# An attention and aggregation kernel over one adjacency: the head's loads and constants placed anew, and the tables of order rewritten

## The chip, the cores and the metric

The kernel runs on one core of a Trainium2 chip. The metric is the device time of one execution in microseconds, the median of several runs. The engines are TensorE (PE in the profile), VectorE (DVE), ScalarE (ACT), GpSimd (POOL) and SyncE (SP). SP only issues DMAs here; ACT and POOL issue DMAs beside their own work. All of them run their own programs in order and wait for each other by semaphores.

## What is computed

There are 4096 nodes with 64 features (`x`), an integer adjacency of 4096 x 4096 (64 MB as it lies in memory), a table of 4096 entities `V` with 64 features, and small matrices. Cut to what matters, the reference is

```python
h = maximum(layernorm(x), 0)
s = h @ W @ a1;  t = V @ W @ a2                 # one number per row, one per column
scores = s[:, None] + t[None, :]
e = where(adj > 0, leaky_relu(scores, 0.2), -9e15)
x = x + elu(softmax(e, axis=1) @ V + h)         # first layer
h = maximum(layernorm(x), 0)
x = x + relu((adj.T @ h) @ U.T / adj.sum(axis=0)[:, None])   # second layer
```

## The kernel before

**Tiling.** The rows of the adjacency are cut into 33 blocks of 124 or 125 rows. They lie on the chip as 8-bit numbers (`adj_sb`), converted by the DMA that loads them. The blocks form five groups, `GROUPS`: (0, 3), (3, 9), (9, 17), (17, 25) and (25, 33). The first layer goes over the groups (stages 0 to 4), and in each over the 32 column chunks `c` of 128. One step `(i, c)` is called a tile here.

**A tile.** PE multiplies the block's chunk by a diagonal matrix of 2^26 with the row's shift below it (`bi`), which is the mask (L1153). On most tiles ACT first writes a relu of the scores into the same PSUM tile (`relu`, L686), PE adds the mask, and ACT takes the exponential (L668). On the tiles in `DVE_TILES` the mask is made alone, DVE joins it with the scores (`scores`, L884), and ACT takes the exponential of that (L672). Two tiles later PE multiplies the exponentials by `V` (`attend`, L1178).

**Guards.** Before a group can start, DVE must find for each of its rows the largest `t` among the row's neighbours: two halves for each block, in `guard` (L832). It reads the adjacency block (semaphore `adj_in[b]`) and `t_row`, which is `t` copied to all partitions. `row_shifts` (L857 to L876) turns the maxima into shifts, PE turns these over (`turn_halves`), ACT copies them (L625), and SP stores them into `bi` by two small DMAs (L372). While stage i runs, DVE makes the guards of group i+1, at the tiles that `GUARD_TILES[i]` names, one entry for each of them. The table `WHEN` names the tile at which every other piece of side work is issued, stage by stage: layer norm of group i+2 (`centre`, `squared`, `variance`, `scaled`), the closing work of group i-1 (`normalise`, `elu`, `square`, `high` and others), and the passing on of `s` (`sum_s`, `turn_s`, `copy_s`). Entries that end in `_0` are for group 1 in stage 0. An engine reaches a piece only after all that its own program has before it.

**The head.** Until the first guard, this runs: SP loads `W`, parts 1 and 3 of `V`, all of `x` and two copies of `U`; ACT loads `a`, and parts 0 and 2 of `V`. DVE forms `W a`, ACT and PE spread it over the partitions (`wa_row`, L599). `V` times that row is formed in four parts, two by POOL (L438) and two by DVE (`weighted`, L777), and DVE sums each (`sum_t`, L787) into `t_col`. PE runs 16 instructions that only keep it busy (L1052) once the first sum is there, and then turns over the smallest `t`, from which the shift comes (`shift_one`, L802 to L811), and makes the eight pieces of `t_row` (L1067); ACT copies six of them and DVE two (L816). DVE runs `centre(0)` (L748 to L752) and `variance(0)` in between. The constants of the mask, the diagonal of 2^26 in `bi` (L741) and in `turn` (L737), are made by DVE at its start.

**The adjacency's loads.** POOL issues them (L417), each behind a fill of the three rows below the block (L413, `set_ones`). It makes five fills first, then its two products for `V`, waits for parts 1 and 3 of `V`, and then issues the loads of blocks 0 to 4. The others follow in six places of POOL's program between other work.

**The second layer.** When the last tile's exponential is done, PE gathers `adj.T @ h` in eleven runs (`gather`, L1239), and DVE divides and adds.

## Time and profile before

| what | value |
|---|---|
| median of 3 runs | 386.7 us (385.74 to 387.5) |
| the profiled execution | 384.23 us |
| its span, first to last instruction | 382.4 us |
| busy: PE / DVE / ACT / POOL | 79% / 77% / 67% / 30% |
| DMA packets | 26809, 25.24 MB written |
| mean granted clock of TensorE | 0.958 of full |

The profile comes from one execution. Its time is 1.8 us more than its span, and 2.5 us below the median of the runs, so a difference is carried over from the profile to the median and not the time itself. A row of the timeline gives start, duration, engine, line, operation, output and inputs, and in square brackets how long the engine had been idle before it and what ended that. A row of the chain of waits gives start, duration and piece. In the rows on the DMA, q0 is POOL's queue, q1 is SP's and q10 is ACT's; the share is the time that its packets took, of 16 DMA engines.

### The profile page before, as it was taken

To read this page: it belongs to the slowest core of one execution; us is meant where nothing else is said; L and a number is where in the kernel's file an instruction comes from. 1 tells how busy PE (TensorE), PEld (TensorE's weight loads), DVE (VectorE), ACT (ScalarE), POOL (GpSimd) and SP (SyncE) were. 2 spreads that over 40 slices of the span, in tenths; PEclk is the share of its full clock that TensorE was granted. 3 is DMA by queue.
4 is the path that set the end of the run, shared out by engine and by line. 5 is a ranking of instruction groups with operands and counts; after the bars stand their busy time and mean duration, and the time that the engine had idled before them with its cause. 6 is when DMAs were issued, how large, how long until landed. Compare 5 with 4: busy or idle time off the path is not lost.

```text
span 382.4 us, 16263 instructions
## 1 busy us (share of the span) xinstructions
PE 302.1 (79%) x7582; PEld 279.3 (73%) x7582; DVE 295.1 (77%) x401; ACT 257.2 (67%) x318; POOL 115.4 (30%) x120
## 2 busy tenths in 40 slices
PE   1916766676778677868788977788989999999996
PEld 0812654576667667767778876678989999999996
DVE  7899999895999578797987798998988764008333
ACT  2312799879999988799989999986787871010000
POOL 8866486387220660030015120012111103010000
PEclk9967699869999999899999999999999999999999
DMA  9999999999999999996000001001110005101100
GB/s 167 135 107 110 108 108 111 137 106 109 110 144 105 102 111 105 101 105 111 3 4 3 3 22 39 2 3 38 26 32 3 3 5 110 30 3 42 34 22 19
DMA packets 26809, 25.24 MB, mean 66 GB/s; under 512 B 22041, under 2 KB 22105, under 8 KB 26742
## 3 DMA queue, kind: packets, MB, share of 16 engines
q0 software_dynamic: 4752, 16.90, 42.5%
q1 hardware_dynamic: 19830, 6.75, 7.9%
q8 instruction: 59, 0.97, 1.0%
q10 hardware_dynamic: 2160, 0.56, 0.8%
q14 instruction: 8, 0.07, 0.0%
HBM read 72.76 MB, written 2.11 MB: 196 GB/s over the span
## 4 chain that ended last, share of the span: by engine, by line
PE 35%; DVE 32%; issue 10%; ACT 10%; POOL 9%; DMA 3%; SPq 0%; POOLq 0%; DVEq 0%; ACTq 0%
DVE scratch L832 20%; PE w L1178 11%; PE q L1239 10%; PE q L1153 6%; PE w L1239 6%; DVE arena L884 5%; ACT q L686 4%; ACT arena L672 3%; ACT arena L668 3%; POOL adj_sb L413 2%; DMA bi<-rows_sb 2%; POOL buf_b L470 2%; POOL adj_sb L417 1%; PE w L1052 1%; POOL stat_c L513 1%
## 5 line engine op out<-in xcount | busy, mean ns | idle before, releaser
L1178 PE MATMUL w<-v_sb,arena 128*61 128x65 f32 (+1 forms) x4224 | 158.0, 225 | 6.7 <-issue 5.4
L832 DVE CUSTOM_DVE_ANT_0 scratch<-adj_sb,t_row 125x2048 uint8<-125x2048 uint8 x66 | 152.5, 2310 | 1.4
L1178 PEld LDWEIGHTS w<-v_sb,arena 128*64 128x64 f32 (+1 forms) x4224 | 143.0, 140 | 8.3 <-issue 6.0
L1153 PE MATMUL q<-bi,adj_sb 128*64 128x125 bf16 x2112 | 95.6, 226 | 45.6 <-ACT q L686 35.8
L1153 PEld LDWEIGHTS q<-bi,adj_sb 128*64 128x64 fp8e4 x2112 | 71.4, 113 | 60.7 <-ACT q L686 46.9
L668 ACT ACTIVATE arena<-q,t_col 128x1000 f32<-128x1000 f32 (+2 forms) x104 | 90.6, 874 | 8.5 <-PE q L1153 8.2
L672 ACT ACTIVATE arena<-arena,t 128x1000 f32<-128x1000 f32 (+2 forms) x56 | 61.3, 1094 | 16.2 <-DVE arena L884 15.5
L884 DVE SCALAR_TENSOR_TENSOR arena<-arena,b_col,q 128x1000 f32<-128x1000 f32 (+1 forms) x42 | 51.0, 1223 | 17.4 <-PE q L1153 13.5
L686 ACT ACTIVATE q<-second_row,minus_b 128x750 f32<-128x750 f32 (+1 forms) x50 | 49.0, 979 | 1.3
L686 ACT ACTIVATE q<-arena,minus_b 128x375 f32<-128x375 f32 (+1 forms) x54 | 43.5, 806 | 1.3
L1239 PE MATMUL q<-g_all,adj_sb 124*128 124x129 f16 (+1 forms) x660 | 39.1, 220 | 0.0
L1239 PEld LDWEIGHTS q<-g_all,adj_sb 124*128 124x128 fp8e4 (+1 forms) x660 | 38.6, 97 | 0.1
L413 POOL MEMSET adj_sb<- 32x1024 f32 x33 | 32.4, 981 | 0.6
L522 POOL TENSOR_TENSOR g_all<-buf_a,g_all 125x512 f16<-125x512 f32 (+2 forms) x5 | 5.4, 1075 | 80.3 <-ACT buf_a L662 80.3
L1239 PE MATMUL w<-g_all,adj_sb 124*128 124x129 f16 (+1 forms) x396 | 23.6, 220 | 0.0
L1019 DVE RECIPROCAL rdeg<-q 128x3 f32<-128x3 f32 (+1 forms) x7 | 1.2, 176 | 29.0 <-PE q L1239 29.0
L1239 PEld LDWEIGHTS w<-g_all,adj_sb 124*128 124x128 fp8e4 (+1 forms) x396 | 23.3, 97 | 0.0
L513 POOL TENSOR_TENSOR stat_c<-stat_b,minus_half 125x8 f32<-125x8 f32 (+2 forms) x5 | 13.1, 2627 | 32.7 <-DVE stat_b L935 32.7
L884 DVE SCALAR_TENSOR_TENSOR arena<-second_row,b_col,q 128x1000 f32<-128x1000 f32 (+1 forms) x14 | 16.4, 1180 | 8.5 <-PE q L1153 4.6
L417 POOL DMA_DIRECT2D adj_sb<-in_adj_dram x33 | 17.9, 545 | 8.3 <-POOL adj_sb L413 8.3
L505 POOL TENSOR_TENSOR buf_a<-x_sb,stat_a 125x512 f32<-125x512 f32 (+2 forms) x5 | 6.6, 1316 | 38.1 <-DVE stat_a L926 38.1
L458 POOL TENSOR_TENSOR stat_c<-stat_b,minus_half 125x8 f32<-125x8 f32 (+2 forms) x5 | 7.2, 1431 | 33.0 <-DVE stat_b L762 33.0
(139 smaller groups left out, 207.2 us busy)
## 6 DMA issues: line engine op xcount, KB each, us to landing
adj_sb<-in_adj_dram POOLq DMA_DIRECT2D x33, 500.0 KB, 40.7
arena<-s_dram SPq DMA_DIRECT2D x2, 500.0 KB, 7.1
out_dram<-v_sb SPq DMA_DIRECT2D x10, 96.0 KB, 1.8
x_sb<-in_x_dram SPq DMA_DIRECT2D x1, 928.0 KB
v_sb<-x_dram SPq DMA_DIRECT2D x1, 768.0 KB, 5.4
v_sb<-n_L_gnn_entity_embs_dram ACTq DMA_DIRECT2D x2, 256.0 KB, 5.7
v_sb<-n_L_gnn_entity_embs_dram SPq DMA_DIRECT2D x2, 256.0 KB, 4.7
second_row<-s_dram SPq DMA_DIRECT2D x1, 500.0 KB, 3.7
```

What stands on the lines that cost most here:

```text
L413: nc.gpsimd.memset(adj_words[96:P, b, :], FOUR_ONES).then_inc(ones_set, 1)
L417: nc.gpsimd.dma_start(adj_sb[0:R, b, :], adj[first_row(b):first_row(b) + R, :]).then_inc(adj_in[b], 16)
L470: nc.gpsimd.tensor_tensor((buf_a if i == 0 else buf_b)[0:R, 0:nb, :], g_sb[0:R, b0:b1, :], wa_row[0:R, 0:1, :].to_broadcast([R, nb, D]), A ...
L513: nc.gpsimd.tensor_tensor(stat_c[0:R, b0:b1], stat_b[0:R, b0:b1], minus_half[0:R, 0:b1 - b0], ALU.pow)\
L668: nc.scalar.activation(e_part(n, nb), part(q[n % Q_SLOTS], nb), ACT.Exp, bias=t_col[:, c:c + 1])\
L672: nc.scalar.activation(e_part(n, nb), e_part(n, nb), ACT.Exp, bias=t02[:, c:c + 1])\
L686: nc.scalar.activation(part(q[n % Q_SLOTS], nb), a_part(i, nb), ACT.Relu, bias=minus_b[:, c:c + 1]).then_inc(relued, 1)
L832: nc.vector.tensor_tensor_reduce(out=junk[0:R, :], in0=adj_bytes[0:R, b, half], in1=t_row[0:R, half], scale=1.0 / ONE, scalar=0.0, op0=ALU ...
L884: nc.vector.scalar_tensor_tensor(out=e_part(n, nb), in0=a_part(i, nb), scalar=b_col[:, c:c + 1], in1=part(q[n % Q_SLOTS], nb), op0=ALU.max ...
L1153: last = nc.tensor.matmul(q[n % Q_SLOTS][e:e + width, bank, start:start + R], weights, bi[:, i % BI_SLOTS, k, :], start=not ON_ACT[n] and ...
L1178: last = nc.tensor.matmul(att(i)[e0:e1, bank, place_in, :], e[:, k * R + e0:k * R + e1], v_sb[:, c, :], start=(c == 0 and place_in == 0), ...
L1239: done = nc.tensor.matmul(out_bank(o)[:, (c - c0) * (2 * D + 1):(c - c0 + 1) * (2 * D + 1)], adj_sb[0:rows, b, c * P:(c + 1) * P], h2[0:ro ...
```

## The change

**Loads of `x`.** `x` has a semaphore for each group. SP loads group 0 first, then `U`, then groups 1 and 3 and the long rows of group 4 (blocks 29 to 32). Group 2 and the rest of group 4 (blocks 25 to 28) are loaded by ACT, which issues these two DMAs after its copies of `t_row`. `centre(i)` waits for its group.

**The constants.** The diagonals of `bi` are made by ACT, behind its copies of `wa_row`; that of `turn` by DVE, after it has split `t`. The copy of the identity to bf16 comes first on DVE.

**`V` times the row.** POOL forms part 0 alone. DVE forms parts 1, 3 and 2, and sums 1, 3, 0, 2 in between. POOL then waits for parts 3 and 2 of `V` and issues the adjacency's loads.

**The shift.** PE multiplies the shift to all partitions after one of the eight pieces of `t_row` and not after two (`SHIFT_AT`).

**The tables.** DVE has three more tiles: (1, 26), (1, 30) and (2, 18). `GUARD_TILES` and `WHEN` are new in a number of places; among them, layer norm of group 2 starts with `centre` at tile 18 of stage 0 and not 8, that of group 1 at tile 7 and not 0, and the scaling of `U` on DVE is at tile 4 and not 7.

```diff
...
     DVE_TILES = [(29, 31),
-                 (25, 27, 29, 31),
-                 (1, 7, 9, 12, 22, 27, 29, 30, 31),
+                 (25, 26, 27, 29, 30, 31),
+                 (1, 7, 9, 12, 18, 22, 27, 29, 30, 31),
                  (1, 3, 6, 8, 10, 12, 28, 29, 30, 31),
...
-    GUARD_TILES = [(7, 8, 10, 11, 12, 15, 15, 16, 18, 19, 20, 22),
-                   (0, 2, 3, 4, 4, 6, 6, 9, 9, 10, 15, 16, 18, 20, 21, 22),
-                   (4, 6, 6, 10, 10, 13, 14, 15, 15, 21, 21, 21, 22, 23, 24, 26),
-                   (4, 9, 10, 12, 13, 17, 17, 17, 17, 19, 21, 21, 21, 23, 23, 24)]
+    GUARD_TILES = [(6, 8, 10, 10, 11, 13, 14, 16, 18, 20, 20, 21),
+                   (0, 0, 2, 3, 4, 6, 6, 11, 11, 13, 15, 18, 20, 20, 21, 23),
+                   (4, 6, 6, 10, 10, 13, 14, 15, 16, 19, 20, 21, 22, 23, 24, 26),
+                   (4, 9, 10, 12, 13, 17, 17, 17, 18, 19, 20, 21, 21, 23, 24, 24)]
...
         'elu': (None, 4, 7, 3, 8),
-        'elu_below': (None, 7, 7, 6, 8),
-        'square': (None, 15, 11, 10, 11),
+        'elu_below': (None, 7, 7, 7, 8),
+        'square': (None, 14, 11, 10, 11),
         'spread': (None, 12, 12, 12, 13),
         'scale': (None, 17, 14, 14, 16),
-        'turn_h2': (None, 20, 17, 18, 18),
+        'turn_h2': (None, 20, 16, 18, 18),
         'copy_h2': (None, 20, 17, 18, 18),
-        'times_u': (None, 22, 19, 25, 21),
+        'times_u': (None, 23, 19, 25, 21),
         'high': (None, 24, 21, 26, 21),
         'sum_s': (11, 2, 4, 2, None),
-        'range': (24, 26, 28, 24, None),
+        'range': (24, 26, 27, 24, None),
         'turn_r': (27, 27, 30, 28, None),
         'copy_r': (27, 27, 29, 27, None),
-        'centre': (8, 1, 3, None, None),
-        'squared': (23, 26, 28, None, None),
+        'centre': (18, 1, 3, None, None),
+        'squared': (24, 26, 28, None, None),
         'variance': (28, 27, 30, None, None),
         'scaled': (31, 30, 31, None, None),
-        'centre_0': (0, None, None, None, None),
-        'squared_0': (1, None, None, None, None),
+        'centre_0': (7, None, None, None, None),
+        'squared_0': (4, None, None, None, None),
         'variance_0': (8, None, None, None, None),
...
         'reduce_v': (3, None, None, None, None),
-        'square_u': (3, None, None, None, None),
-        'scale_u': (7, None, None, None, None),
+        'square_u': (2, None, None, None, None),
+        'scale_u': (4, None, None, None, None),
         'turn_u': (1, None, None, None, None),
-        'copy_u': (2, None, None, None, None),
+        'copy_u': (4, None, None, None, None),
         'turn_s': (13, 11, 9, 10, None),
-        'copy_s': (15, 7, 19, 12, None),
+        'copy_s': (15, 10, 19, 12, None),
     }
...
     TINY = 1e-30
+    SHIFT_AT = 1
...
     T_ON_ACT, T_ON_DVE = (0, 2, 4, 5, 6, 7), (1, 3)
-    LN_PARTS = [(0, 1), (1, 9), (9, 17), (17, 25), (25, 33)]
...
         v_in = [sem(f"v_in{i}") for i in range(PARTS)]
-        x_in = sem("x_in")
+        x_in = [sem(f"x_in{i}") for i in range(NI)]
+        bi_set = sem("bi_set")
...
             load_v(3)
-            sp.dma_start(x_sb[:, 0:SHORT, :], x_short).then_inc(x_in, 16)
-            sp.dma_start(x_sb[0:R, SHORT:NB, :], x[EDGE:N, :].rearrange("(k p) d -> p k d", p=R)).then_inc(x_in, 16)
+            def load_x(i):
+
+                b0, b1 = GROUPS[i]
+                sp.dma_start(x_sb[:, b0:b1, :], x_short[:, b0:b1, :]).then_inc(x_in[i], 16)
+
+            load_x(0)
             for h in range(2):
                 sp.dma_start(u_sb[:, h * D:(h + 1) * D], U[:, :]).then_inc(u_in, 16)
+            for i in (1, 3):
+                load_x(i)
+            sp.dma_start(x_sb[0:R, SHORT:NB, :], x[EDGE:N, :].rearrange("(k p) d -> p k d", p=R)).then_inc(x_in[NI - 1], 16)
...
                 elif b == ONES_FIRST:
-                    pool.wait_ge(v_weighted_pool, 2)
+                    pool.wait_ge(v_weighted_pool, 1)
                 elif b == 7:
...
             pool.wait_ge(ones_set, ONES_FIRST)
-            for k in (0, 2):
-                chunks = slice(k * NC // PARTS, (k + 1) * NC // PARTS)
-                pool.wait_ge(v_in[k], 16)
-                pool.wait_ge(wa_rows_copied, 2)
-                if k == 0:
-                    pool.wait_ge(consts, 6)
-                else:
-                    pool.wait_ge(v_weighted_pool, 1)
-                nc.gpsimd.tensor_tensor(v_wa[:, chunks, :], v_sb[:, chunks, 0:D],
-                                        wa_row[:, 1:2, :].to_broadcast([P, NC // PARTS, D]), ALU.mult).then_inc(v_weighted_pool, 1)
-            for k in (1, 3):
+            chunks = slice(0, NC // PARTS)
+            pool.wait_ge(v_in[0], 16)
+            pool.wait_ge(wa_rows_copied, 2)
+            pool.wait_ge(consts, 6)
+            nc.gpsimd.tensor_tensor(v_wa[:, chunks, :], v_sb[:, chunks, 0:D],
+                                    wa_row[:, 1:2, :].to_broadcast([P, NC // PARTS, D]), ALU.mult).then_inc(v_weighted_pool, 1)
+            for k in (3, 2):
                 pool.wait_ge(v_in[k], 16)
...
                     .then_inc(wa_rows_copied, 1)
+            act.wait_ge(consts, 2)
+            act.wait_ge(consts_dve, 2)
+            for s in range(BI_SLOTS):
+                nc.scalar.activation(bi[0:R, s, :, :], ident[0:R, 0:R].unsqueeze(1).to_broadcast([R, 8, R]), ACT.Copy, scale=BIG)\
+                    .then_inc(bi_set, 1)
             act.wait_ge(t_summed, PARTS)
...
                     .then_inc(t_copied_act, 1)
+            for i, (b0, b1) in ((2, GROUPS[2]), (4, (GROUPS[4][0], SHORT))):
+                act.dma_start(x_sb[:, b0:b1, :], x_short[:, b0:b1, :]).then_inc(x_in[i], 16)
...
                 act.wait_ge(shifts_turned, 1)
+                act.wait_ge(bi_set, BI_SLOTS)
                 nc.scalar.activation(bi[96:P, 0, 0:nb, :].rearrange("p b c -> p (b c)"), first_rows()[96:P], ACT.Copy)\
...
             dve.wait_ge(consts, 2)
-            nc.vector.tensor_scalar(turn[0:R, 0:3, 0:29], ident[0:R, 96:R].unsqueeze(1).to_broadcast([R, 3, 29]), BIG, None, ALU.mult)\
-                .then_inc(consts_dve, 1)
-            dve.wait_ge(consts_dve, 3)
-            for s in range(BI_SLOTS):
-                nc.vector.tensor_scalar(bi[0:R, s, :, :], ident[0:R, 0:R].unsqueeze(1).to_broadcast([R, 8, R]), BIG, None, ALU.mult)\
-                    .then_inc(consts_dve, 1)
+            nc.vector.tensor_copy(ident16[:, :], ident[:, :]).then_inc(consts_dve, 1)
...
                 mean, part_x = stat_a[0:R, b0:b1], x_sb[0:R, b0:b1, :]
+                dve.wait_ge(x_in[i], 32 if i == NI - 1 else 16)
                 nc.vector.tensor_reduce(mean, part_x, AX.X, ALU.add).then_inc(sum1_done, 1)
...
                 chunks = slice(k * NC // PARTS, (k + 1) * NC // PARTS)
-                if k % 2 == 1:
-                    dve.wait_ge(v_weighted_dve, k // 2 + 1)
+                if k == 0:
+                    dve.wait_ge(v_weighted_pool, 1)
                 else:
-                    dve.wait_ge(v_weighted_pool, k // 2 + 1)
+                    dve.wait_ge(v_weighted_dve, {1: 1, 3: 2, 2: 3}[k])
                 nc.vector.tensor_reduce(t_col[:, chunks], v_wa[:, chunks, :], AX.X, ALU.add).then_inc(t_summed, 1)
...
-            nc.vector.tensor_copy(ident16[:, :], ident[:, :]).then_inc(consts_dve, 1)
             weighted(1)
+            sum_t(1)
+            weighted(3)
+            sum_t(3)
+            weighted(2)
             sum_t(0)
-            weighted(3)
-            sum_t(1)
             sum_t(2)
-            sum_t(3)
             dve.wait_ge(t_summed, PARTS)
...
             nc.vector.tensor_tensor(t_lo, t_col[:, :], t_hi, ALU.subtract).then_inc(t_split, 1)
+            nc.vector.tensor_scalar(turn[0:R, 0:3, 0:29], ident[0:R, 96:R].unsqueeze(1).to_broadcast([R, 3, 29]), BIG, None, ALU.mult)\
+                .then_inc(consts_dve, 1)
             dve.wait_ge(t_min_turned, 1)
...
                                            op0=ALU.mult, op1=ALU.max).then_inc(shift_one_done, 1)
-            dve.wait_ge(x_in, 32)
             centre(0)
...
             pe.wait_ge(t_split, 1)
-            pe.wait_ge(consts_dve, 2 + 1 + BI_SLOTS + 1)
+            pe.wait_ge(consts_dve, 3)
             for g in range(NG):
-                if g == 2:
+                if g == SHIFT_AT:
                     pe.wait_ge(shift_one_done, 1)
...
                 pe.wait_ge(a_copied, 1)
+                pe.wait_ge(consts_dve, 4)
                 nb = GROUPS[0][1] - GROUPS[0][0]
...
                     pe.wait_ge(bi_made, 1)
+                    pe.wait_ge(bi_set, BI_SLOTS)
                 if c == 0 and i >= 1:
...
                 if ON_ACT[n]:
...
```

## Rows read from the trace of the kernel before

**Rows 1.** The page: shares of the chain that ended last, by engine.
```profile
PE 35%; DVE 32%; issue 10%; ACT 10%; POOL 9%; DMA 3%; SPq 0%; POOLq 0%; DVEq 0%; ACTq 0%
```

**Rows 2.** Busy time by stretch: length, then PE, PEld, DVE, ACT, POOL, clock, DMA.
```profile
160.00:180.00 20.00, 15.61 (x441) 13.92 (x438) 18.37 (x19) 19.26 (x21) 3.26 (x1) 1.00 0.91 112
```

**Rows 3.** The chain of waits, the head: start, length, piece.
```profile
4.97 1.86 DVE bi L741 x2
...
10.22 3.79 PE w L1052 x16
...
15.19 1.02 DVE stat_a L750
...
19.04 2.29 DVE scratch L832
```

**Rows 4.** Timeline of DVE in the head.
```profile
8.89 0.68 DVE L777 TENSOR_TENSOR arena<-v_sb,wa_row 128x512 f32<-128x512 f32 x1
...
10.09 1.06 DVE L777 TENSOR_TENSOR arena<-v_sb,wa_row 128x512 f32<-128x512 f32 x1
11.08 1.86 DVE L787 TENSOR_REDUCE t_col<-arena 128x8 f32<-128x512 f32 x3
12.97 0.19 DVE L797 TENSOR_REDUCE columns<-t_col 128x1 f32<-128x32 f32 x1
```

**Rows 5.** Timelines of ACT, POOL and SP in the head.
```profile
1.36 1.48 ACTq L575 DMA_DIRECT2D v_sb<-n_L_gnn_entity_embs_dram  x2
...
6.44 0.34 ACT L599 ACTIVATE wa_row<-w 128x64 f32<-128x64 f32 x2 [1.26 <-PE w L1047]
...
26.36 0.48 ACT L631 ACTIVATE arena<-w 128x375 f32<-128x375 f32 x1 [5.90 <-PE w L1125]
...
7.40 1.49 POOL L438 TENSOR_TENSOR arena<-v_sb,wa_row 128x512 f32<-128x512 f32 x1
...
10.55 2.84 POOL L417 DMA_DIRECT2D adj_sb<-in_adj_dram  x5
...
3.81 5.79 SPq L353 DMA_DIRECT2D x_sb<-in_x_dram  x1
```

**Rows 6.** DMA: q1 in 10 to 11 us; q0 and q1 in 18 to 20 us.
```profile
q1 hardware_dynamic: 851, 0.22, 134.1%
...
q0 software_dynamic: 54, 0.20, 97.7%
q1 hardware_dynamic: 53, 0.01, 4.9%
```

**Rows 7.** DMA issues, us to landing: block 0 alone, then the first five (median).
```profile
adj_sb<-in_adj_dram POOLq DMA_DIRECT2D x1, 500.0 KB, 8.2
...
adj_sb<-in_adj_dram POOLq DMA_DIRECT2D x5, 500.0 KB, 17.3
```

**Rows 8.** Timeline of DVE: two guards, block 2's first and the ninth of stage 0.
```profile
29.23 2.29 DVE L832 CUSTOM_DVE_ANT_0 scratch<-adj_sb,t_row 125x2048 uint8<-125x2048 uint8 x1
...
60.86 2.29 DVE L832 CUSTOM_DVE_ANT_0 scratch<-adj_sb,t_row 125x2048 uint8<-125x2048 uint8 x1
```

**Rows 9.** Timelines of DVE and ACT: the end of stage 1.
```profile
125.14 1.00 DVE L884 SCALAR_TENSOR_TENSOR arena<-second_row,b_col,q 128x750 f32<-128x750 f32 x1 [0.37 <-PE q L1159]
...
127.31 0.27 ACT L625 ACTIVATE rows_sb<-w 16x125 bf16<-16x125 f32 x1
```

**Rows 10.** The chain of waits, the end of stage 1.
```profile
128.34 5.97 DMA bi<-rows_sb
```

**Rows 11.** Timelines of ACT and DVE, stage 2.
```profile
169.66 1.10 ACT L686 ACTIVATE q<-arena,minus_b 128x1000 f32<-128x1000 f32 x1
170.70 1.08 ACT L668 ACTIVATE arena<-q,t_col 128x1000 f32<-128x1000 f32 x1
...
183.66 1.13 ACT L672 ACTIVATE arena<-arena,t 128x1000 f32<-128x1000 f32 x1
...
182.29 1.26 DVE L884 SCALAR_TENSOR_TENSOR arena<-arena,b_col,q 128x1000 f32<-128x1000 f32 x1 [2.83 <-PE q L1153]
```


## The prediction, made before the changed kernel had run

> **What bounds the kernel now.** I read the chain of waits first, then the head's timelines, then the busy time by stretch, then the queues. The chain goes through PE and DVE for two thirds of its length [rows 1], and no stage in it is free: the head runs on DVE and PE to 19.0, where the first guard starts [rows 3]; stages 0 and 1 follow DVE's guards; in stage 2 ACT is busy for 19.26 of 20 us [rows 2]; the end is PE's. So time saved early counts only if DVE, the adjacency and ACT all let it through.
>
> In the head, DVE makes the two diagonals of `bi` from 4.97 on [rows 3], though `wa_row` is there by 6.8 [rows 5], and weighs its first part of `V` only at 8.89 [rows 4]. The last sum ends at 12.94 and the smallest `t` is taken at 12.97. PE's 16 filler instructions start at 10.22 and take 3.79 [rows 3], so PE can turn over the smallest `t` only at 14.0. A stop of DVE follows, the mean of `x` at 15.19 with 1.02 us for 125x3 elements [rows 3].
>
> The loads have a timetable of their own. Block 0 is issued at 10.55 [rows 5] and lands 8.2 later, at 18.8; the median of the first five is 17.3 us [rows 7], which is block 2, issued about 11.7 and so landing about 29.0. DVE asks for block 2 at 29.23 [rows 8]. So in group 0 guards and loads arrive together: a faster DVE alone gains nothing there.
>
> **DVE's part of the head.** What goes from DVE's start: 2.88 us of diagonals, of which the chain shows 1.86 before the work behind it. What comes: one product for `V`, at 0.68 to 1.06 us [rows 4]. The new order from 6.85 is product 1, sum 1, product 3, sum 3, product 2, sum 0, sum 2. Three products at 0.68 and four sums at 0.62 (1.86 for three [rows 4]) are 4.5 us, so the smallest `t` starts at 11.4 and not 12.97, if nothing stops DVE. If product 3 has to wait until POOL's product ends at 8.9 [rows 5], 0.7 is added and it is 12.1. PE's filler starts after sum 1, at about 8.2, and ends at 12.0, not 14.0. PE can thus turn `t` over at 12.0 to 12.5, 1.3 to 1.8 earlier. Behind that DVE has the diagonal of `turn`, a few tenths, partly in its wait for PE. The shift is multiplied after one piece of `t_row`; it was behind the mean of `x` anyway, so this is worth nothing by itself. The mean can again stop for up to 1 us: POOL's second fill behind the loads falls at about 13.7, where the mean stands now. I take the stop as it was; without it 0.9 more comes. First guard: 1.4 earlier, at 17.6 (bounds 0.7 and 2.2).
>
> The one-microsecond stop ends where POOL's fill ends, as the trace has it. The Trainium skill, SBUF — State Buffer, section on the two separate sides, says that VectorE and GpSimd share one pair of ports as an exclusive lock, also for a VectorE operation with two SBUF inputs against a GpSimd one that reads SBUF. By that rule a second VectorE product beside POOL's waits it out whole, and the smallest `t` starts at 12.1; the trace agrees only in part (one product took 0.68 beside POOL's, one took 1.06 [rows 4]).
>
> **ACT's part.** Two diagonals on ACT: 2 x 1.1 us, estimated by the 128x1000 relu at 1.10 [rows 11], from 6.8 to 9.0. The next thing there waits for the sums, beyond 11.4, so they cost nothing; if the cover were gone, their 2.2 us would stand before the first guard. Two DMA issues come after the copies of `t_row`: two of twice the size together took 1.48, but SP was once held for 5.79 by one issue [rows 5]. ACT's next wait, for PE and the first row of scores, was 5.90 long [rows 5] and keeps that length, so both ends fit and I cost it at nothing; `copy_rows` and everything else of ACT is queued behind it.
>
> **The loads.** POOL drops its second product, 1.5 us, and issues from about 9.0, 1.6 earlier than 10.55 [rows 5]. Parts 2 and 3 of `V` were used before the first loads were issued and are not later now. SP keeps 2804 packets behind `V` (group 0, `U`, groups 1 and 3, the long rows) where there were 4340. At 851 in a microsecond [rows 6] the 1536 missing ones are 1.8 us of the queue, so SP's share is done when the adjacency begins. Blocks 0 and 2 land at 17.2 and 27.4.
>
> The 1536 packets come back beside the adjacency. In 18 to 20 us POOL's queue moved 54 packets and SP's 53 [rows 6]: they alternate, and SP's took 4.9% of 16 engines, 0.030 us each (0.049 x 2 x 16 / 53). From about 20 to 27 that is some 190 packets, 0.35 us on block 2. It lands at 27.8, and DVE wants it at 29.23 - 1.4 = 27.8. Group 0 so ends 1.2 to 1.4 earlier, and the load of block 2 is late next. Later blocks have over a microsecond to spare, also with the 2.9 us (1536 x 0.030 / 16) that the small packets take in all.
>
> **Stage 0.** Of its side work only the order changes: one `centre` of eight blocks moves from before guard 5 to behind guard 9, `U` is scaled before the first guard, where DVE may wait some 0.1 for POOL. The sum for DVE is the same. I carry 1.4 to stage 1 (bounds 0.7 and 2.2).
>
> **Stage 1.** ACT is relieved of two tiles, but DVE's guards set its end, and one score of 1.00 us (tile 26) now stands between the last guard and `row_shifts`. DVE had 0.37 of idle just behind them [rows 9]. The copy of the shifts on ACT at 127.31 [rows 9] and SP's small DMA of 5.97 us [rows 10] hang on this. Bounds: the whole 1.00 is lost, or nothing. I take 0.5 as lost, between the 0.63 that this idle leaves and the ease that ACT gets in front of its copy: 0.9 is left at the start of stage 2.
>
> **Stage 2.** Tile 18 falls where ACT is full. There it costs relu and exponential, 1.10 + 1.08; afterwards only 1.13 [rows 11]: 1.05 less. DVE has 1.26 more and had 2.83 of idle before tile 22 [rows 11]. The last guards start behind tile 22, so they come 1.0 earlier too (bounds: nothing, if PE was what held tile 22, and 1.1). The rest of the tables shifts entries by a tile or two; nothing for it, bounds 0.5 either way. Stages 3 and 4 and the gather keep their length.
>
> **Sum.** 1.4 - 0.5 + 1.0 = 1.9 us. The profiled execution would be 382.3 instead of 384.2; on the median, 386.7 - 1.9 = 384.8.
>
> **Rivals.**
> 1. *Group 2's `x` lands late* (slower). Its 1024 packets alternate with the adjacency's from about 20. `centre(2)` stands behind the ninth guard, which ended at 63.15 [rows 8]; less 1.4 and less the 1.5 of the moved `centre` that is 60.3. At 27 packets in a microsecond [rows 6] they need 38 us, landing at 58; it decides against the change when the rate is under 1024 / 40 = 25. At 22 it lands at 66.5 and DVE stands for 6.2 us with all guards of group 1 behind it: 386.7 - 1.9 + 6.2 = 391.0; at 24, 2.4 us more and 387.2. At 23, 4.2 more: 389.0, which I take as its price. For it: there is hardly any reserve, and the last of 16 engines counts. Against it: 53 beside 54.
>    The Trainium skill, DMA: Bandwidth & Descriptors, section on queues, rings and completion order, says that each engine goes round the queues packet by packet; the trace agrees (53 beside 54). By it the rate is that of the adjacency's packets, and `x` is in time.
> 2. *The head's gain is lost before stage 2.* Stage 1 loses the whole 1.0, or blocks 1 and 2 come later, since the early rows of `x` also delay them; what is left is stage 2's 1.0 and a few tenths: 385.8. For it: DVE and loads are level in group 0, and the 5.97 us of the small DMA vary.
> 3. *More than the sum.* The mean of `x` is not stopped, stage 1 loses nothing: 2.2 + 1.0 + 0.4 of the tables: 383.1.
> 4. *ACT is held by its two issues* for longer than 5.9 us. Against it: 1.48 for twice as many packets. It would end as rival 2 or slower.
>
> **Chances.** Forecast 0.47, rival 1 0.13, rival 2 0.22, rival 3 0.15, rival 4 0.03. What a measurement of this kernel can tell from no change is 0.5%, 1.9 us: faster is below 384.8. The forecast lies on that line, and I give it 0.29 to faster and 0.18 to same; with rival 3 faster is 0.44. Same: 0.18, rival 2 and 0.01 of rival 4, 0.41. Slower: rival 1 and the rest, 0.15. The range goes from 382.7 (rival 3 with its bounds) to 388.4 (rival 1 for the greater part).
>
> **What the profile would show.** The first product for `V` on DVE near 6.9; the smallest `t` at 11.4 to 12.3; the filler on PE at 8.2; the first adjacency issue at 9.0, landing by 17.3; the first guard at 17.6 and block 2's at 27.8. ACT's wait before its first copied row stays over 3 us. No idle of DVE before `centre(2)` near 60, else rival 1. Tile (1, 26)'s score before `row_shifts`, and the copy of shifts near 126.4, else rival 2. Tile 22 of stage 2 some 2 us earlier. The prediction is wrong if the first guard does not move by a microsecond, or if a gain that is there at stage 2 is gone at the gather.

## The result and the profile after

The changed kernel takes 387.38 us (median of 22 runs, 385.57 to 388.71), the kernel before 385.95 beside it (22 runs, 383.62 to 387.5). The ratio is 1.0034, with a 95% interval of 1.0019 to 1.005: slower by 1.4 us. 384.8 was predicted, 1.9 us less than the 386.7 of before from which the prediction started. The profiled execution took 387.07 us, its span is 385.3. The one of before was itself 1.7 us under its median of 22 runs; a second trace of that kernel was of an execution of 387.09, so single traces of it differ by 2.9 us. What the second trace was expected to show:

> The kernel before, unchanged, for a second trace: the first was 1.7 us faster than the median of its kernel. All theories expect the same times to about 0.2 us at the first guard (19.0) and at the start of stage 1, and 0 to 2.5 us later at the end of stage 2 (the last row_shifts of stage 2 at 194 to 196.5), Theory C in the form of longer idle of TensorE by issue (7.4 us in 36 to 206 in the first trace, 9 to 12 here).

It came out so: first guard at 19.03, the last `row_shifts` of stage 2 at 195.69, and 11.8 us of "issue", where the first trace has 7.7.

The page of after, the busy time of each engine and the shares of the chain that ended last:

```profile
PE 302.0 (78%) x7590; PEld 279.0 (72%) x7590; DVE 295.4 (77%) x403; ACT 256.5 (67%) x317; POOL 113.2 (29%) x119
...
PE 38%; DVE 24%; ACT 20%; issue 8%; DMA 5%; POOL 4%; SPq 1%; DVEq 0%; POOLq 0%
```

No engine has notably less or more to do. DVE's share of the chain is 24% where it was 32% [rows 1], ACT's 20% where it was 10%; but the second trace of before has 21% and 20%, so this can't be put down to the change.

The head's times are near the predicted ones. After, timeline of DVE from the first product to the first guard:

```profile
6.35 0.69 DVE L785 TENSOR_TENSOR arena<-v_sb,wa_row 128x512 f32<-128x512 f32 x1 [1.34 <-DMA v_sb<-n_L_gnn_entity_embs_dram]
7.08 0.69 DVE L795 TENSOR_REDUCE t_col<-arena 128x8 f32<-128x512 f32 x1
8.66 0.69 DVE L785 TENSOR_TENSOR arena<-v_sb,wa_row 128x512 f32<-128x512 f32 x1 [0.89 <-DMA v_sb<-n_L_gnn_entity_embs_dram]
...
11.89 0.19 DVE L805 TENSOR_REDUCE columns<-t_col 128x1 f32<-128x32 f32 x1
12.00 0.81 DVE L806 CAST scratch<-t_col 128x32 bf16<-128x32 f32 x1
...
13.99 0.59 DVE L758 TENSOR_SCALAR stat_a<-stat_a 125x3 f32<-125x3 f32 x1
...
17.42 2.29 DVE L841 CUSTOM_DVE_ANT_0 scratch<-adj_sb,t_row 125x2048 uint8<-125x2048 uint8 x1
```

The first product starts at 6.35, where it was 8.89 [rows 4]; the smallest `t` at 11.89, where it was 12.97; the first guard at 17.42, where it was 19.04 [rows 3]. POOL's fill, at 11.82 for 0.95, now falls beside the cast at 12.00, which takes 0.81. After, timelines of POOL, ACT and PE in the head:

```profile
8.94 2.84 POOL L425 DMA_DIRECT2D adj_sb<-in_adj_dram  x5 [0.72 <-DMA v_sb<-n_L_gnn_entity_embs_dram]
...
6.13 1.97 ACT L608 ACTIVATE bi<-ident 125x1000 bf16<-125x1000 f32 x2
...
17.47 0.37 ACTq L621 DMA_DIRECT2D x_sb<-in_x_dram  x1
...
17.88 0.62 ACTq L621 DMA_DIRECT2D x_sb<-in_x_dram  x1
...
24.74 0.48 ACT L643 ACTIVATE arena<-w 128x375 f32<-128x375 f32 x1 [5.90 <-PE w L1135]
...
7.82 3.78 PE L1061 MATMUL w<-ident 128*128 128x128 f32 x16 [1.95 <-DVE t_col L795]
```

The adjacency's first load goes out at 8.94. ACT's diagonals end at 8.1, its two issues took 0.99 us, and its wait is still 5.90. Rival 4 is out.

**Where the lead goes.** The start of a group's `row_shifts` on DVE (L857 before, L866 after) marks the end of its guards. From the timelines of DVE, us:

| kernel | first guard | group 0 | group 1 | group 2 | group 3 |
|---|---|---|---|---|---|
| before | 19.04 | 33.90 | 70.20 | 123.33 | 194.06 |
| before, second trace | 19.03 | 34.12 | 70.47 | 123.57 | 195.69 |
| after | 17.42 | 32.25 | 68.92 | 123.46 | 196.92 |

The lead of 1.6 is still 1.3 to 1.5 when stage 0 ends. It is gone at the end of stage 1, and stage 2 is 1.3 to 2.7 us longer. Tile 22 of stage 2, which should have come 2 us earlier, is 2.9 later than in the first trace of before and 1.4 later than in the second (183.76). After, timeline of DVE at the end of stage 1, then at tile 22 of stage 2:

```profile
121.50 2.04 DVE L893 SCALAR_TENSOR_TENSOR arena<-second_row,b_col,q 128x750 f32<-128x750 f32 x2
123.46 0.16 DVE L866 TENSOR_TENSOR g_max<-g_max 125x8 f32<-125x8 f32 x1
...
185.16 1.26 DVE L893 SCALAR_TENSOR_TENSOR arena<-arena,b_col,q 128x1000 f32<-128x1000 f32 x1 [1.96 <-PE q L1164]
```

The two scores in front of `row_shifts` are those of tiles 25 and 26. The score at 185.16 waited for PE. What did PE wait for? The waits of PE from 138 to 182 us (columns: engine and line, releaser, us in all, times, the longest), first before:

```profile
PE w L1178 <- issue: 4.8, 4, 2.0
PE q L1153 <- ACT q L686: 3.5, 6, 1.0
PE q L1153 <- issue: 1.1, 2, 0.8
```

and after:

```profile
PE w L1189 <- issue: 4.8, 4, 2.6
PE q L1164 <- ACT q L698: 4.7, 6, 1.5
PE w L1216 <- DVE rows_sb L858: 2.0, 1, 2.0
PE q L1164 <- issue: 0.4, 1, 0.4
```

In before, 5.9 of the 9.4 us in which PE stood are "issue": nothing that the profile records held it. In after it is 5.2, and the 2.0 before L1216, which have DVE's name, turn out below to be of the same kind. The stops come some 6 us apart, also inside a tile. Before, timeline of PE: 32 equal matmuls of one `attend`, of which the last 19 come 2 us late:

```profile
154.63 0.78 PE L1178 MATMUL w<-v_sb,arena 128*64 128x65 f32 x19 [2.00 <-issue]
```

The DMA view has a queue of its own kind for this. From 96 to 187 us its line is the same before and after (packets, MB, share of 16 engines):

```profile
q8 instruction: 16, 0.26, 1.0%
```

These are 16 packets of 16 KB in 91 us. From 96 to 182 us PE ran 1865 matmuls and 1861 weight loads in before; over 15 packets that is 250 instructions a packet, so q8 brings PE's program. The starts of its packets, from the trace, in us from the span's start:

| kernel | 4th | 6th | 21st | mean distance, 6th to 21st |
|---|---|---|---|---|
| before | 65.9 | 85.5 | 176.6 | 6.08 |
| before, second trace | 65.9 | 85.6 | 178.0 | 6.16 |
| after | 62.3 | 85.1 | 177.1 | 6.13 |

The expectation for the changed kernel with the wide mask, further down, has the packets of 96 to 182 us; it counts from the start of the DMA record, 10.5 to 10.6 us before the first instruction. The 4th packet comes 3.6 us earlier after the change, the 6th 0.4. From there to the end of the adjacency's load (its last packet starts at 179) they come about 6.1 us apart; behind that, the 22nd to 28th of before are 3.3 to 5.3 apart.

Do these packets end PE's stops? The longest stop of each trace, and the one that has DVE's name:

| kernel | PE stood for | a packet of q8 ended | PE went on |
|---|---|---|---|
| before | 2.00 (issue) | 153.41 | 154.63 |
| before, second trace | 2.27 (issue) | 154.90 | 156.25 |
| after | 2.56 (issue) | 153.57 | 155.06 |
| after | 2.02 (`<-DVE rows_sb`) | 178.03 | 179.28 |

It is so for all of them. The traces of before, after and experiments 1 to 4 have 71 "issue" stops from 36 to 206 us, and each ends 1.20 to 1.59 us behind the end of a packet of q8. PE's waits of over 0.8 us for ACT or for the row's DMA, in the same traces from 119 to 190 us, end 4.8 to 6.3 us behind one. So PE stands there until its next instructions are in.

When does this bind? In those seven traces no "issue" stop before 119 us is longer than 0.2 us, though the packets come as far apart; from 119 to 186 us, the end of stage 1 and stage 2, there are up to 12 in a trace. This is theory C, on which the experiments turn, as far as the traces bear it: in stage 2 the supply of PE's instructions sets a pace that neither head nor tables can beat, while new delays are added to it. Stage 1 is not paced by it.

The Trainium skill, Runtime: NRT & Kernel Launch, section on instruction fetch mechanics, says that an engine fetches blocks of 256 instructions through a DMA queue of its own while it runs the present block, and that the crossing is mostly hidden. The blocks are there in the trace; hidden they are not, beside the adjacency's load, at 5.9 us in the 44 from 138 to 182 us.

### The profile page after: what moved, and what is told of

It is laid out like the page before. It is cut to its first block, busy times and chain, and to the rows that moved or that the text cites. A ratio compares the mean times of both kernels' runs of the same rounds, so it can differ in the third digit from the quotient of the medians.

```text
span 385.3 us, 16284 instructions
## 1 busy us (share of the span) xinstructions
PE 302.0 (78%) x7590; PEld 279.0 (72%) x7590; DVE 295.4 (77%) x403; ACT 256.5 (67%) x317; POOL 113.2 (29%) x119
## 4 chain that ended last, share of the span: by engine, by line
PE 38%; DVE 24%; ACT 20%; issue 8%; DMA 5%; POOL 4%; SPq 1%; DVEq 0%; POOLq 0%
DVE scratch L841 14%; PE w L1189 11%; PE q L1250 10%; ACT q L698 9%; ACT arena L680 8%; PE q L1164 7%; PE w L1250 6%; DVE arena L893 5%; DMA bi<-rows_sb 4%; ACT arena L684 3%; DMA v_sb<-n_L_gnn_entity_embs_dram 2%; PE w L1085 2%; POOL stat_c L517 1%; PE w L1216 1%; POOL stat_c L462 1%
## 5 line engine op out<-in xcount | busy, mean ns | idle before, releaser
L680 ACT ACTIVATE arena<-q,t_col 128x1000 f32<-128x1000 f32 (+2 forms) x101 | 87.8, 872 | 7.9 <-PE q L1164 7.8
L684 ACT ACTIVATE arena<-arena,t 128x1000 f32<-128x1000 f32 (+2 forms) x59 | 64.2, 1089 | 22.0 <-DVE arena L893 21.3
L893 DVE SCALAR_TENSOR_TENSOR arena<-arena,b_col,q 128x1000 f32<-128x1000 f32 (+1 forms) x43 | 52.3, 1224 | 20.1 <-PE q L1164 15.1
L698 ACT ACTIVATE q<-second_row,minus_b 128x750 f32<-128x750 f32 (+1 forms) x48 | 47.2, 983 | 1.3
L698 ACT ACTIVATE q<-arena,minus_b 128x375 f32<-128x375 f32 (+1 forms) x53 | 42.4, 800 | 1.2
L893 DVE SCALAR_TENSOR_TENSOR arena<-second_row,b_col,q 128x1000 f32<-128x1000 f32 (+1 forms) x16 | 18.4, 1156 | 7.9 <-PE q L1164 4.6
L517 POOL TENSOR_TENSOR stat_c<-stat_b,minus_half 125x8 f32<-125x8 f32 (+2 forms) x5 | 13.1, 2617 | 31.4 <-DVE stat_b L944 31.4
L462 POOL TENSOR_TENSOR stat_c<-stat_b,minus_half 125x8 f32<-125x8 f32 (+2 forms) x5 | 9.1, 1821 | 34.3 <-DVE stat_b L770 34.3
```

Source lines behind the costliest of these rows:

```text
L462: nc.gpsimd.tensor_tensor(stat_c[0:R, b0:b1], stat_b[0:R, b0:b1], minus_half[0:R, 0:b1 - b0], ALU.pow)\
L517: nc.gpsimd.tensor_tensor(stat_c[0:R, b0:b1], stat_b[0:R, b0:b1], minus_half[0:R, 0:b1 - b0], ALU.pow)\
L680: nc.scalar.activation(e_part(n, nb), part(q[n % Q_SLOTS], nb), ACT.Exp, bias=t_col[:, c:c + 1])\
L684: nc.scalar.activation(e_part(n, nb), e_part(n, nb), ACT.Exp, bias=t02[:, c:c + 1])\
L698: nc.scalar.activation(part(q[n % Q_SLOTS], nb), a_part(i, nb), ACT.Relu, bias=minus_b[:, c:c + 1]).then_inc(relued, 1)
L893: nc.vector.scalar_tensor_tensor(out=e_part(n, nb), in0=a_part(i, nb), scalar=b_col[:, c:c + 1], in1=part(q[n % Q_SLOTS], nb), op0=ALU.max ...
```

## The experiments

**Without the wide mask.** All four ran beside each other and 35 runs of before (385.92 us).

1. `copy_s` of stage 2 earlier, for the stop of 2.0 us above, where PE seems to wait for DVE's copy into `rows_sb`:

```diff
-        'copy_s': (15, 10, 19, 12, None),
+        'copy_s': (15, 10, 15, 12, None),
```

> The changed kernel with one entry moved: the copy of s for group 3 stands at tile 15 of stage 2 and not at 19, so ahead of the guard at 16, the new VectorE tile 18 and the guard at 19. Theory A (VectorE reaches that copy late; TensorE stands 2.02 us at times_u for it and then runs at half clock, with all of stage 2 behind): the wait is gone and tile 22 comes about 2.9 us earlier than in the changed kernel; 387.4 - 2.9 = 384.5 us, ratio to before 0.995 to 0.998. Theory B (the rows of x loaded beside the adjacency make the later loads and the small DMAs slow, and the loss sits there): nothing moves, ratio 1.002 to 1.005.

Measured: 387.58 us, 1.0029 (1.0002 to 1.0055), as the change. DVE's copy now ended at 172.62 and no longer at 178.65. Its timeline of PE:

```profile
181.01 0.92 PE L1216 MATMUL w<-uu,buf_b 128*125 128x128 f32 x6 [2.05 <-issue]
```

The stop stays and changes its name. It ends 1.24 us behind a packet of q8, as it did in the changed kernel; the releaser named there was only the last to arrive that the view shows. Theory A fell.

2. Tile 18 of stage 2 back on ACT:

```diff
-                 (1, 7, 9, 12, 18, 22, 27, 29, 30, 31),
+                 (1, 7, 9, 12, 22, 27, 29, 30, 31),
```

> The changed kernel with tile (2, 18) back on ScalarE, all else kept, the guard at tile 19 too. Theory A: VectorE loses the 1.66 us wait and the 1.25 us score in front of the copy of s, which ends near 175.8 and not 178.7, before TensorE wants it at 177.3; ScalarE has its 1.05 us back. 387.4 - 2.9 + 1.05 = 385.5, ratio 0.998 to 1.000. Theory B: no better than the changed kernel, and worse by ScalarE's 1.05: ratio 1.003 to 1.007.

Measured: 386.63 us, 1.0000 (0.9975 to 1.0025). The tile was predicted as a gain of 1.0; taking it back gives 0.75, with intervals that overlap. It is no gain here. The ratio is one that theory A gave, whose mechanism experiment 1 had just taken away.

3. The new head and the new stage 0, with the entries of stages 1 to 4 as before:

```diff
-                 (25, 26, 27, 29, 30, 31),
-                 (1, 7, 9, 12, 18, 22, 27, 29, 30, 31),
+                 (25, 27, 29, 31),
+                 (1, 7, 9, 12, 22, 27, 29, 30, 31),
...
-        'copy_s': (15, 10, 19, 12, None),
+        'copy_s': (15, 7, 19, 12, None),
```

> The new head with the new entries of stage 0, and the tables of stages 1 to 4 as before. Theory A: what the head gives (1.6 us at the first guard, of which the trace still has 0.4 to 1.3 in stage 1) arrives: 384.7 to 385.6, ratio 0.9965 to 0.999. Theory B: the head's gain is eaten by slower DMAs: ratio 1.000 to 1.004.

Measured: 386.35 us, 1.0004 (0.9977 to 1.0031). The head alone moves nothing.

4. The code of before with all new tables (`DVE_TILES`, `GUARD_TILES`, `WHEN`):

```diff
-                 (25, 27, 29, 31),
-                 (1, 7, 9, 12, 22, 27, 29, 30, 31),
+                 (25, 26, 27, 29, 30, 31),
+                 (1, 7, 9, 12, 18, 22, 27, 29, 30, 31),
...
-        'centre': (8, 1, 3, None, None),
+        'centre': (18, 1, 3, None, None),
...
```

> The kernel before with the new tables alone: head, loads and constants as before. Theory A: the whole loss of stage 2 without the head's gain, 1.0 to 2.9 us: ratio 1.003 to 1.0075. Theory B: the tables are harmless: ratio 0.998 to 1.002.

Measured: 387.82 us, 1.0051 (1.0023 to 1.0079). The tables carry the loss.

**Fewer instructions of PE.** One number halves the mask's matmuls in stages 1 and 2: for each block one with 128 columns of weights and not two with 64. It was put into both kernels:

```diff
-    MASK_COLUMNS = (64, 64, 64, 64, 64)
+    MASK_COLUMNS = (64, 128, 128, 64, 64)
```

> The changed kernel with the mask of stages 1 and 2 multiplied 128 columns at a time and not 64: TensorE has 60 and not 72 instructions for a tile of stage 1 and 80 and not 96 for one of stage 2. Theory C: while the adjacency is loaded, a page of 256 TensorE instructions arrives only each 6.1 us (the instruction queue's packets in the traces of before and after lie 6.07 and 6.14 us apart from 96 to 182 us, and 4.6 to 4.7 apart later), TensorE stands idle for 0.4 to 2.6 us at the page's end, and what the other engines gain is taken back there. Then fewer instructions free stage 2: its idle by issue (5 to 10 us in the traces so far) falls below 2 us, 387.4 - 3 to - 5 = 382.4 to 384.4, ratio 0.990 to 0.996, and the head's gain shows against the next kernel. Theory A (VectorE reaches the copy of s late): ratio stays 1.002 to 1.005.

> The kernel before with the same wider mask in stages 1 and 2. Theory C: it also gains, by less than the changed kernel, as it starts 1.6 us later: 385.9 - 1.5 to - 3.5, ratio 0.991 to 0.996, and 1 to 1.6 us above the run before this. Theory A, or a TensorE that is slower with wide weights: ratio 1.000 or more, and the run before this is 1.4 us above it, as without the wide mask.

Measured: the changed kernel 382.45, 0.9918 (0.9898 to 0.9939); before 381.20, 0.9882 (0.9865 to 0.9899). Both gain, as theory C had it; but before was expected 1 to 1.6 us above the changed kernel and is 1.25 below, so no gain of the change was hidden. Before with this mask, the waits of PE from 138 to 182 us, all of them:

```profile
PE q L1153 <- ACT q L686: 6.0, 12, 1.0
```

Every "issue" stop is gone; from 86 to 177 us q8's packets are 5.7 to 8.1 us apart, 6.9 in the mean, so PE asks for them more slowly than it did. Is it the supply, or does the wide mask save PE's own time? The same width in all stages:

```diff
-    MASK_COLUMNS = (64, 64, 64, 64, 64)
+    MASK_COLUMNS = (128, 128, 128, 128, 128)
```

> Before with 128 columns of weights for the mask in all stages, not in 1 and 2 alone. Theory C (TensorE's instructions are fetched too slowly while the adjacency loads, until about 182 us): in stage 0 DVE's guards set the pace and in stages 3 and 4 the loading is over, so it gains little on the 0.9882 of stages 1 and 2 alone: 0.986 to 0.988. Rival (the wide mask saves TensorE's own time, whatever the fetch): stages 3 and 4, where TensorE is on the path, gain as much again as stages 1 and 2 did: 0.976 to 0.982.

Measured: 389.01 us, 1.0073 (1.0048 to 1.0097), 8 us over the version above. Both expectations missed. Busy time by stretch (PE first, instructions in brackets), in stage 1, before and then with the mask wide in stages 1 and 2:

```profile
96.00:123.00 27.00, 20.55 (x582) 17.98 (x578) 26.65 (x30) 26.26 (x37) 6.33 (x3) 1.00 1.00 120
```

```profile
96.00:123.00 27.00, 22.65 (x487) 18.57 (x488) 26.65 (x29) 26.42 (x37) 6.29 (x3) 1.00 1.01 120
```

In stage 3, with the mask wide in stages 1 and 2:

```profile
190.00:260.00 70.00, 56.98 (x1692) 52.38 (x1688) 61.99 (x76) 63.94 (x67) 14.96 (x10) 1.00 0.04 11
```

and in all stages:

```profile
190.00:260.00 70.00, 60.62 (x1422) 52.87 (x1418) 61.37 (x78) 63.49 (x66) 15.11 (x10) 1.00 0.03 10
```

PE is busy 3.6 us longer with 270 matmuls fewer, and 2.1 us longer with 95 fewer in stage 1. The wide mask costs PE time of its own in both, so it doesn't gain by saving PE's work: the rival of theory C is out. It gains in stage 2 alone (67.0 and 68.3 us in two traces, where the two of before have 70.7 and 72.1), and not in stage 1 (53.4 where it was 53.1). Of the 6.7 us between the two traces 0.6 are lost in stage 3 and 5.8 behind it, in stage 4 and the gather.

**With the wide mask: is the change worth something once PE is fed?**

The head and stage 0 (as 3, and the mask), then the tables alone (as 4, and the mask):

> The new head and stage 0 with the tables of stages 1 to 4 as before, and the mask of stages 1 and 2 made with 128 columns of weights a matmul in place of two of 64. Without the stops of TensorE's instruction supply, the old head and old tables gave a ratio of 0.9882, the whole change 0.9918. Theory D (the head is a gain that the supply hid): 1.0 to 1.5 us under that version of before, a ratio of 0.984 to 0.986. Rival (the packets of x beside the adjacency cost at the small DMA into bi what the head gained): 0.3 us under to 0.5 over it, 0.987 to 0.990. If it is 0.991 or more, the new head itself is the loss.

> The code of before with all the new tables, and the same wide mask. Theory D: the tables carry the whole penalty of some 1.3 us and more, since a faster head has to be made good too: 1.3 to 2.6 us over before with the wide mask, a ratio of 0.9915 to 0.995. Rival (the tables cost only through the supply of instructions): 0.988 to 0.990, as before with the wide mask.

Measured: 381.81, 0.9892 (0.9864 to 0.9919), and 383.02, 0.9922 (0.9895 to 0.9949). The first falls on its rival, a head that is worth nothing, the second on theory D, tables that cost. The changed kernel with the mask and tile 18 back on ACT, and before with the mask and two tiles of stage 1 on DVE:

> The changed kernel with the wide mask (0.9918) and tile 18 of stage 2 back on ScalarE. Theory F (the tile on VectorE delays the copy behind it, for which TensorE waits 1.0 us at the product with U): that wait is gone and it gains 0.4 to 1.0 us, a ratio of 0.989 to 0.9907. Rival (without the stops of the supply the tile is a gain, as the prediction had it, since ScalarE sets the pace of stage 2): it loses 0.3 to 1.0 us, 0.9925 to 0.9945.

```diff
-                 (25, 27, 29, 31),
+                 (25, 26, 27, 29, 30, 31),
```

> Before with the wide mask (0.9882) and tiles 26 and 30 of stage 1 moved to VectorE, no other entry. Theory G: the score of tile 26 stands between the last guard and the shifts of the next row, so that these start 0.7 to 1.0 us later and stage 2 as much later: 0.990 to 0.9908. Rival (stage 2 takes its pace from elsewhere, or ScalarE's relief pays it back): 0.9875 to 0.989.

Measured: 381.90, 0.9909 (0.9878 to 0.9941), and 382.50, 0.9918 (0.9887 to 0.995), the first between its two sides, the second over both. Last, stage 2's entries alone, the same with the new head, and the mask alone again:

```diff
-                 (1, 7, 9, 12, 22, 27, 29, 30, 31),
+                 (1, 7, 9, 12, 18, 22, 27, 29, 30, 31),
...
-        'turn_h2': (None, 20, 17, 18, 18),
+        'turn_h2': (None, 20, 16, 18, 18),
...
-        'range': (24, 26, 28, 24, None),
+        'range': (24, 26, 27, 24, None),
```

> Before with the wide mask of stages 1 and 2 and the new entries of stage 2 alone (tile 18 to VectorE, the guards of group 3, two steps one tile earlier). Theory: without the stops of the supply ScalarE and VectorE set stage 2's pace, as the prediction had it, and the entries are worth the 0.6 us by which stage 2 was shorter in the traces with all new tables (66.5 against 67.1 us): 0.4 to 1.0 us under before with the wide mask, which runs beside it. Rival: nothing, within 0.2 per cent of it.

> The same with the new head and the new stage 0: the change without its entries of stages 1, 3 and 4. Theory (the head keeps 0 to 0.7 us of its lead at stage 1, the two tiles of stage 1 were the loss): 0 to 0.7 us under the version without the new head, the best of all. Rival (blocks and x of group 2 arrive too late for the head to pay at all): equal to it or up to 0.6 us over.

> Before with the wide mask of stages 1 and 2 once more, as the measure for the two beside it, in more rounds: 0.987 to 0.990 of before.

Measured: 381.55, 0.9906 (0.9872 to 0.9939); 382.33, 0.9903 (0.9873 to 0.9934); 382.09, 0.9909 (0.9879 to 0.9938; 0.987 to 0.990 was expected). All these lie between 381.2 and 383.0, and nearly all of their intervals overlap: the wide mask is worth some 1%, and no part of the change can be told from nothing on top of it. In the first pair the change was 1.25 us slower than before also with the mask; the repeat of before (382.09 after 381.20) takes most of that back. Before with the mask beats before by 0.9 to 1.2%, and the changed kernel by more, and nothing beside it was measurably faster.

The traces say more than the times. Ends of the guards as in the table above, and the distance from group 1 to group 2 (stage 1) and from 2 to 3 (stage 2):

| kernel, with the mask | first guard | group 1 | stage 1 | stage 2 |
|---|---|---|---|---|
| before | 19.49 | 70.65 | 53.40 | 67.04 |
| new head and stage 0 | 17.57 | 70.42 | 53.39 | 67.31 |
| two tiles of stage 1 | 18.84 | 70.50 | 54.27 | 66.77 |
| tables alone | 19.01 | 70.41 | 54.43 | 66.44 |
| the change | 17.44 | 70.11 | 54.89 | 66.59 |
| the change, tile 18 back | 17.02 | 69.51 | 54.26 | 68.02 |
| before, a second measurement | 19.36 | 70.49 | 53.36 | 68.28 |
| stage 2's entries alone | 19.03 | 70.18 | 53.09 | 66.30 |
| the same with the new head | 19.04 | 70.44 | 53.37 | 68.39 |

*Stage 1.* The two tiles alone make it 0.87 us longer. DVE with the mask alone, then with the two tiles:

```profile
123.14 0.99 DVE L884 SCALAR_TENSOR_TENSOR arena<-second_row,b_col,q 128x750 f32<-128x750 f32 x1
124.05 0.16 DVE L857 TENSOR_TENSOR g_max<-g_max 125x8 f32<-125x8 f32 x1
```

```profile
122.96 1.90 DVE L884 SCALAR_TENSOR_TENSOR arena<-second_row,b_col,q 128x750 f32<-128x750 f32 x2
124.77 0.16 DVE L857 TENSOR_TENSOR g_max<-g_max 125x8 f32<-125x8 f32 x1
```

One score more stands before the shifts, and its whole length is lost. The other traces bear it out: stage 1 takes 54.2 to 55.4 us in the eight that have the two tiles, with and without the mask, and 53.1 to 53.4 in the eight others of this table, of before and of experiment 3.

*Stage 2.* With PE fed, the change has a stage 2 that is 1.4 us shorter than with tile 18 back on ACT (66.59 against 68.02). But two traces of one kernel, before with the mask, differ by as much (67.04 and 68.28), and the fourth with the tile on DVE has 68.39. The mean of the four with it is 66.9, that of the five without 67.5. A gain of some half a microsecond may be there; the predicted 1.05 is not shown, nor is any in the time.

*The head.* Its lead is 1.9 at the first guard and 0.2 at group 1. The trace of the version with head and stage 0 shows one cause, on DVE:

```profile
61.41 0.69 DVE L756 TENSOR_REDUCE stat_a<-x_sb 125x8 f32<-125x512 f32 x1 [0.66 <-DMA x_sb<-in_x_dram]
```

`centre(2)` waits 0.66 us for its `x`, in experiment 1 0.45 at 62.08; in the six other traces with the new head and the new stage 0 it did not wait. Elsewhere blocks came late. Experiment 3, timeline of DVE:

```profile
17.09 2.29 DVE L841 CUSTOM_DVE_ANT_0 scratch<-adj_sb,t_row 125x2048 uint8<-125x2048 uint8 x1 [1.37 <-DMA adj_sb<-in_adj_dram]
...
23.18 2.29 DVE L841 CUSTOM_DVE_ANT_0 scratch<-adj_sb,t_row 125x2048 uint8<-125x2048 uint8 x1 [0.50 <-DMA adj_sb<-in_adj_dram]
```

**Does `x` have to be moved at all?** First, experiment 3 with all of `x` issued by SP ahead of the adjacency, in pieces:

```diff
-            for i in (1, 3):
+            for i in (1, 2, 3):
                 load_x(i)
+            sp.dma_start(x_sb[:, GROUPS[4][0]:SHORT, :], x_short[:, GROUPS[4][0]:SHORT, :]).then_inc(x_in[4], 16)
...
-            for i, (b0, b1) in ((2, GROUPS[2]), (4, (GROUPS[4][0], SHORT))):
-                act.dma_start(x_sb[:, b0:b1, :], x_short[:, b0:b1, :]).then_inc(x_in[i], 16)
```

> The new head with stages 1 to 4 as before (1.0004 when last run), but all of x is issued by SyncE in the head: nothing of x is loaded beside the adjacency. If the 1536 small packets beside the adjacency cost what was lost between the first guard (1.6 us early) and the start of stage 1 (0.35 to 0.5 early), 0.9 us comes back at the small DMA into bi: ratio 0.998. If the early start of the adjacency is worth more, the first two blocks land up to 1.8 us later and VectorE waits for block 1 or 2: ratio 1.000 to 1.003. Theory C: whichever of these holds at stage 1 is levelled in stage 2, ratio 0.999 to 1.001.

Measured: 401.23 us (394.14 to 407.48; before 385.76 beside it), 4% slower, and its two fastest runs are still 2.6% slower (1.0257, 1.0217 to 1.0298). None of the expected ratios held. Its chain of waits:

```profile
57.05 27.56 DMA s_dram<-rows_sb
84.61 0.02 issue
84.62 9.76 DMA second_row<-s_dram
```

SP's small store of stage 1's row took 27.56 us, in SP's queue behind packets of `x` that were still there: 159 small packets of q1 in the 27 us from 57 to 84. Then the new head with SP's loads and all tables as before, and the wide mask:

```diff
+            sp.dma_start(x_sb[:, 0:SHORT, :], x_short).then_inc(x_in[0], 16)
+            sp.dma_start(x_sb[0:R, SHORT:NB, :], x[EDGE:N, :].rearrange("(k p) d -> p k d", p=R)).then_inc(x_in[0], 16)
```

> The new head on ScalarE, VectorE and GpSimd, but x loaded by SyncE in one piece behind V, as before, and all tables as before; the mask of stages 1 and 2 with 128 columns, to compare with 0.9882 (before with that mask) and 0.9892 (the new head with the new stage 0 and that mask). Theory E: the head's lead was lost in stage 0, because the mean of x for group 2 had to go behind the ninth guard, and GpSimd's power of group 1 then stands beside a guard of VectorE and takes 3.29 us in place of 1.33. With the mean back in front, the power takes 1.3 to 1.7, stage 1 begins 1.2 to 1.8 us earlier, and the time is 1.0 to 1.6 us less than before with the mask: 0.984 to 0.9856. Rival: the lead is lost to the loads, which begin beside the packets of x: the first guards of group 0 wait for adjacency blocks by 1 us or more, and the ratio is 0.987 to 0.990; if the store of stage 1's row lands over 10 us after its issue, over 1.0.

Of its 12 runs seven took 406 to 416 us and five 382.8 to 384.3; the ratio of the five is 0.9946 (0.9914 to 0.9978). The trace is of one of the seven. DVE, at the mean of `x` in the head:

```profile
48.75 0.35 DVE L747 TENSOR_REDUCE stat_a<-x_sb 125x3 f32<-125x192 f32 x1 [34.53 <-DMA x_sb<-in_x_dram]
```

and its queues from 14 to 42 us:

```profile
q0 software_dynamic: 822, 2.90, 99.2%
q1 hardware_dynamic: 355, 0.09, 2.3%
```

355 of SP's packets take 28 us, and `x` lands behind still more of them. The first load went out at 9.46 here, at 10.55 in before [rows 5]. One wait more holds it back:

```diff
             for k in (3, 2):
                 pool.wait_ge(v_in[k], 16)
+            pool.wait_ge(v_weighted_dve, 3)
```

> The version with the new head and x loaded in one piece as before (first adjacency load issued at 9.46, where before issues it at 10.55), with one wait more: GpSimd issues the first load only when VectorE's third product of V is done, at about 11.2. Theory H (an adjacency load that starts while the packets of x are still queued leaves some engines with one packet of x for each long one of the adjacency, and x lands 30 us late): with the loads held x lands by 15 us, no run is over 390 us, the first guard waits for block 0 until 19.3 to 19.7, and the time is that of before with the wide mask, 380.5 to 383.5 us. Rival (the late landing comes from something else in the new head): again more than a third of the runs over 395.

Measured: 382.31 us, 0.9901 (0.9867 to 0.9935), no run over 383.1; `x` by 15 and no run over 390 is what theory H had. The timelines of POOL and DVE:

```profile
11.20 2.84 POOL L418 DMA_DIRECT2D adj_sb<-in_adj_dram  x5 [2.58 <-DVE arena L777]
...
13.82 0.35 DVE L748 TENSOR_REDUCE stat_a<-x_sb 125x3 f32<-125x192 f32 x1 [0.80 <-DMA x_sb<-in_x_dram]
...
19.16 2.29 DVE L833 CUSTOM_DVE_ANT_0 scratch<-adj_sb,t_row 125x2048 uint8<-125x2048 uint8 x1 [1.41 <-DMA adj_sb<-in_adj_dram]
```

`x` is there at 13.8, and the first guard is as late as in before, since it waits for block 0. With the loads early and `x` in one piece seven of 12 runs take over 400 us, with the loads held the lead is gone. So the split of `x` is what lets the head go earlier safely, and without it there is nothing to gain: either loads or `x`.

## Why the prediction was wrong

**The head: right, in part by errors that cancel.** First guard at 17.42 (17.6), smallest `t` at 11.89 (11.4 to 12.3), filler at 7.82 (8.2), first issue at 8.94 (9.0); ACT's part and its two issues cost nothing. The products began 0.5 earlier than in the working, and product 3 then waited 0.89 for its part of `V`, a wait that the working doesn't have. POOL's fill cost the cast 0.64 more (0.81, before 0.17) and the mean of `x` 0.42 less (0.59, before 1.01). And the first guard is at 17.0 to 17.6 in only six of the eight traces with the new head, at 18.6 and 19.0 in the others.

**Rival 1: its mechanism, at its edge.** After, the queues from 30 to 36 us:

```profile
q0 software_dynamic: 174, 0.62, 98.4%
q10 hardware_dynamic: 172, 0.04, 5.2%
```

29 packets of `x` in a microsecond, one for one with the adjacency's, where 25 was the break-even. `centre(2)` at 60.40 has no idle; in two of eight traces it waited 0.45 and 0.66. The cost is tenths and not 4.2.

**Group 0: level, as said, and now one, now the other is late.** Blocks held the guards of group 0 back in four of eight traces with the new head, by 1.1 to 2.3 us in all, and in two of nine with the old one, by 0.3 and 1.7. Of the 1.4 to be carried to stage 1 the mean shows 0.6 to 0.7: group 1 ends at 69.8 in those eight, with and without mask, and at 70.5 in the nine.

**Stage 1: mis-sized.** 0.5 was taken as lost, with the bound 1.0. The two tiles cost 0.87 alone, and in the change stage 1 was 54.54 us long and not 53.13: 1.4 lost, beyond the bound. ACT's relief did not shorten DVE's line.

**Stage 2: the step that failed.** The sum gave tile 18 a gain of 1.05, because ACT was busy for 19.26 of 20 us [rows 2]. In its place the stage was 73.46 us long and not 70.73 or 72.12, 1.3 to 2.7 longer, at the pace of PE's instructions. The row on ACT did not carry the step: the stretch before it, in the same trace, and the same stretch in the second trace of before are

```profile
140.00:160.00 20.00, 15.50 (x432) 14.46 (x430) 17.10 (x18) 16.54 (x17) 1.39 (x2) 0.91 0.98 105
```

```profile
160.00:180.00 20.00, 14.37 (x404) 12.81 (x398) 17.01 (x18) 17.52 (x19) 3.26 (x1) 1.00 0.84 90
```

with ACT at 16.54 and 17.52. [rows 1] hinted at it, "issue" at 10% of the chain, and [rows 2] too, with PE busy for 15.6 of 20 and ACT waiting on what PE makes; I read the busiest engine as the bound and did not follow the engine that stood.

The same pace swallows the head. Experiment 3, which has the head and not the two tiles, enters stage 2 at 122.50, 0.8 to 1.1 earlier than before, and leaves it at 196.37, 0.7 to 2.3 later. Rival 2 has the head's gain lost, but kept stage 2's 1.0 and gave 385.8, 0.9 under before; here both are lost, by a mechanism that it did not name. The measured 387.38 lies in the range, whose upper end, 388.4, was there for rival 1: that is luck.

**Why slower, and not the same.** The tables alone cost 0.5%, and the head without them is worth nothing. The two tiles' 0.9 us is shown where PE is fed. What places the rest is argued only: delays of stage 1 and stops such as that at L1216 come on top of the supply's pace. Experiment 2, which keeps the two tiles and gives up tile 18 alone, is level with before, so even the share of the two tiles in the 1.4 us is open. The stops in PE's supply also spread the traces: they sum to 7.7 us in one trace of before from 36 to 206 us, to 11.8 in the other, to 8.8 in after, to 12.0 to 13.0 in experiments 1 to 3 and to 9.5 in experiment 4.

A rival stands beside them untested, the clock granted to TensorE. Right behind the stop that ends at 154.63 it is at 0.66 of full in the mean of 155 to 160 us, so for part of that time at 1.2 and not 2.4 GHz. Over stage 2 the mean is 0.98 in both traces of before (70.7 and 72.1 us), 0.95 in after (73.5), experiment 3 (73.9) and experiment 4 (72.9), and 1.00 in experiment 1 (71.5). What the lower level costs by itself, and what is the stops' own, no run here separates.

**Something unforeseen in stage 0, without a price.** POOL's power for group 1, before, then after, on POOL's timeline:

```profile
43.24 1.33 POOL L458 TENSOR_TENSOR stat_c<-stat_b,minus_half 125x6 f32<-125x6 f32 x1 [5.44 <-DVE stat_b L762]
```

```profile
42.04 3.29 POOL L462 TENSOR_TENSOR stat_c<-stat_b,minus_half 125x6 f32<-125x6 f32 x1 [7.14 <-DVE stat_b L770]
```

It stood beside `centre(2)` and now stands beside a guard, and ends 1.2 us behind that guard's end at 44.1. It starts 1.2 earlier and ends 0.8 later. DVE's wait behind it stayed at 0.82 us, with one more guard in front, so it cost no time of its own. In the last two kernels of the experiments, where the mean is back in front, it takes 1.33 again, and nothing is gained by it; the prediction has nothing on it.

**Open.** Why the instruction packets come 6.1 us apart beside the load, and what makes up the 1.4 us by which the change is slower, is not settled.

## What to carry to other kernels

Where PE is not busy and the engine it seems to wait for isn't free either, look at "issue" among its waits and at the instruction queue in the DMA view before costing an edit, and ask whether each stop ends just behind a packet of it: a stretch that is paced by instruction supply returns nothing for a faster head or a moved tile, but fewer instructions there (here half the mask's matmuls, some 1%) pay at once. A busy share from one stretch of one trace is no bound; a second trace of the same kernel had ACT at 17.5 us where the first had 19.3. A step of score that is moved in front of a hand-over counts in full. And an earlier start of a bulk load is only safe when the small packets ahead of it are through, or moved beside it in a queue that nobody waits for.

## What was not expected of the hardware

- PE's instructions come in packets of 16 KB through a DMA queue, 6.1 us apart while the adjacency loads and down to 3.3 us apart behind it; PE stood for up to 2.6 us at one of them, and went on 1.20 to 1.59 us behind the packet's end.
- A mask of 128 columns a matmul costs PE more time than two of 64: 60.62 us busy with 1422 matmuls against 56.98 with 1692, in the same 70 us.
- One us in the start of a bulk load can decide over 30: with the load issued at 9.46 `x` landed at 48.7, and seven of 12 runs took over 400 us; at 10.55 (before) and 11.20 none did. The Trainium skill, DMA: Bandwidth & Descriptors, section on queues, rings and completion order, has each engine go round its queues packet by packet, which agrees with 174 beside 172. That only some engines keep such packets is what 355 of them beside 822 suggest; it wasn't measured.
- The small DMA into `bi` for group 1 took 6.37 us after, 6.14 in experiment 3, with packets of `x` still under way, and 5.30 in the second trace of before.
